# Attention and expert layer on one core: queries of head 0 issued ahead of two adjacency loads, and the shift rows and sums of unit 1 ahead of key copies

## The chip, the cores and the metric

The kernel runs on one core of a Trainium2 chip. The metric is the device time of one execution in microseconds (us). Five queues of instructions run side by side: TensorE (PE), VectorE (DVE), ScalarE (ACT), GpSimd (POOL) and SyncE (SP). They meet at semaphores only. SP does nothing here but wait for semaphores and issue DMAs, one after the other.

## The reference

The first half of the reference is a graph attention over 2048 nodes with 8 heads of 32 dimensions, masked by a 2048 x 2048 adjacency matrix:

```python
hs = layer_norm(h_source, ln1_scale, ln1_bias)
ht = layer_norm(h_target, ln1_scale, ln1_bias)
q = (ht @ Wq + bq).reshape(T, H, HD) / jnp.sqrt(jnp.float32(HD))
k = (hs @ Wk + bk).reshape(S, H, HD)
v = (hs @ Wv + bv).reshape(S, H, HD)
logits = jnp.einsum('thd,shd->hts', q, k)
logits = jnp.where(edge_mask[None] != 0, logits, NEG)
probs = jax.nn.softmax(logits, axis=-1)
ctx = jnp.einsum('hts,shd->thd', probs, v).reshape(T, D)
```

An output projection, a layer norm and a feed-forward layer follow, then a second residual layer that sends each node to two of eight experts. The change touches none of these.

## The kernel before

**Stages.** A front stage (0 to about 104 us) loads and normalises the inputs, turns them, and projects keys, queries and values in groups of 512 columns. Then 32 attention units run, one for a block of 512 target rows and a head: `n = 8 * b + h`. After them come projection, feed-forward and the experts.

**What a unit needs.** Queries and keys are kept as a high and a low part, stacked as three bands of 32 partitions, so that one matmul of 96 rows gives a score of nearly full precision: `ks` holds the keys of all heads, `qs` the queries of four units (a ring of 4). `piece` (L1575) computes scores target by source, from which DVE takes the row maxima (L973, with the mask `maskA`) and ACT the row sums (L1398). Maxima and sums of a unit are turned by TensorE (`turn_negmax`, L1584), split by DVE (`turned_shift`, L942 to L947), and stored by SP as two more rows of `qs`: `store_shift` (L433). Then `key_scores` (L1598, L1600) computes scores source by target with these rows as a bias and with the mask `maskB` added by a matmul with an identity, ACT takes the exponential (L1484), and `add_context` (L1612) multiplies by the values. The pieces of unit n+2 run between the key scores of unit n, and the key scores of a unit wait for its shift rows: `shift_rows[h % 4]` (L1590).

**SP's order.** It is written out by hand in `sync`: what stands late in it waits for everything before it. The helpers named below are:

- `stack_keys(h, cols, which)`: copies of 32 partitions from `kq_hi`, `kq_lo` into `ks` (L401).
- `stack_query(h)`: three copies of the queries of block 0 into `qs` (L407). The first for head 0 waits for `kq_split`, the ninth split by DVE (L920).
- `next_adjB(h)` and `load_adjB(b, h)`: 512 KB of the transposed adjacency into one of two buffers (L426). For h of 2 and more it waits until POOL has read the buffer: `maskB_next`.
- `store_queries`, `load_q`: queries of later blocks to DRAM and back (L414, L419).
- `store_shift`, `store_sums`, `load_inv`: the shift rows, the inverse sums to DRAM, and these back to 64 partitions (L433, L446, L454). `load_inv(n)` waits for `context_scaled >= n + 1`, POOL's multiplication for unit n-1.

In unit n the loop loads the queries of unit n+3, the adjacency of unit n+9 (after `maskB_next >= n + 8`), stores the context of unit n-2, and then does the three of unit n+1.

**POOL's order.** In unit n it makes the mask of block b+1 (`mask_b`, L725), scales the context of unit n-1 (L731), and prepares a chunk of the experts' weights (L700 to L712). `mask_b(1, 0)` waits for all key copies (`k_out`), because block 1's masks lie where the keys were made, and for its adjacency load.

Of the kernel before, what the change touches and what calls it, by code (L numbers as in the profile page):

```python
# [31 lines left out]
def graph_attention_and_experts(nc, x, adj, adjT, nodemask, h_target, ln1_scale, ln1_bias, Wq, bq, Wk, bk, Wv, bv,  # L32
                                Wo, bo, ln2_scale, ln2_bias, W1, W2, gate_wT, w1T, b1, w2T, b2, out):
    T, D = x.shape
    NT = T // P
    DC = D // P
    H = 8
# [5 lines left out]
    NG = NT // GT  # L43
    QSCALE = float(HD) ** -0.5
    KR = 3 * HD
    F = W1.shape[1]
    FC = F // P
    E, _, HE = w1T.shape
    HC = HE // P

    ctx = ExitStack()
    with ctx:
        def sem(name):
            return ctx.enter_context(nc.semaphore(name))
# [92 lines left out]
        kq_split = sem("kq_split")  # L147
# [51 lines left out]
        N = NB * H  # L199
# [28 lines left out]
        maskB_next = sem("maskB_next")  # L228
# [157 lines left out]
        with block:  # L386
            @block.sync
            def _(sp):
# [7 lines left out]
                def stack_keys(h, cols, which=(0, 1, 2)):  # L396
                    c, at_ = h // HPC, h % HPC * HD
                    for r in which:
                        part_ = (kq_hi, kq_lo, kq_hi)[r]
                        done = k_out[min(h, 2) if h < 4 or r == 1 else 3]  # L400
                        sp.dma_start(ks[r * HD:(r + 1) * HD, h, cols].bitcast(F32),  # L401
                                     part_[at_:at_ + HD, c, cols].bitcast(F32)).then_inc(done, 16)

                def stack_query(h):
                    at_ = h * HD
                    for r in range(3):
                        sp.dma_start(qs[r * HD:(r + 1) * HD, h, :].bitcast(F32),  # L407
                                     qq[at_:at_ + HD, 0, r // 2, 0, :].bitcast(F32)).then_inc(q_in[h], 16)

                def store_queries(g):  # L410
                    for c in range(DC):
                        sp.wait_ge(kq_split, DC * (NG + g) + c + 1)
                        for r, rows_ in enumerate((qh_rows, ql_rows)):
                            sp.dma_start(rows_[c * P:(c + 1) * P, g * GP:(g + 1) * GP],  # L414
                                         qq[:, g % 2, r, c, :].bitcast(F32)).then_inc(q_out[g % 2], 16)

                def load_q(n, b, h):
                    for r, rows in enumerate((q_high, q_high, q_low)):
                        sp.dma_start(qs[r * HD:(r + 1) * HD, h % 4, :].bitcast(F32),  # L419
                                     rows[h, :, bass.ds(b * TB, TB)]).then_inc(q_in[h % 4], 16)  # L420

                def load_adjA(tile, a):
                    sp.dma_start(adjA[:, a % 2, :], adj_t[tile, :, :]).then_inc(adjA_in[a % 2], 16)

                def load_adjB(b, h):
                    sp.dma_start(adjB[:, h % 2, :, :], adjT_t[:, 2 * h:2 * h + 2, bass.ds(b * TB, TB)])\  # L426
                        .then_inc(adjB_in[h % 2], 16)

                def store_shift(n, h):

                    sp.wait_ge(shift_split, n + 1)
                    for r, rows in enumerate((shift_hi, shift_lo)):
                        sp.dma_start(qs[KR + r:KR + r + 1, h % 4, :].bitcast(F32), rows[:, h % 2, :].bitcast(F32))\  # L433
                            .then_inc(shift_rows[h % 4], 16)

                def store_context(n, b, h):

                    wait_apart(sp, context_scaled, n + 2)
                    for half in range(2):
                        sp.dma_start(ctx_out[h, :, bass.ds(b * TB + half * (TB // 2), TB // 2)],  # L440
                                     total[half * HD:(half + 1) * HD, h % 2, :])\
                            .then_inc(context_out[h % 2], 16)

                def store_sums(n, h):
                    wait_apart(sp, inv_turned, n + 1)
                    sp.dma_start(inv_rows[bass.ds(n, 1), :].rearrange("o (a p) -> (o a) p", p=P),  # L446
                                 inv_sb[:, h % 2, :]).then_inc(sums_out[h % 2], 16)

                def load_inv(n, b, h):

                    sp.wait_ge(sums_out[h % 2], 16 * (b * (H // 2) + h // 2 + 2))
                    sp.wait_ge(context_scaled, n + 1)
                    for half in range(2):
                        sp.dma_start(rT[half * HD:(half + 1) * HD, :],  # L454
                                     inv_rows[bass.ds(n, 1), half * (TB // 2):(half + 1) * (TB // 2)]
                                     .rearrange("o t -> (o t)").partition_broadcast(HD)).then_inc(inv_in, 16)
# [14 lines left out]
                def load_h(b):  # L471
                    sp.dma_start(hb[:, b, :, :], ht_rows[b * TB:(b + 1) * TB, :]
                                 .rearrange("(a p) d -> p a d", p=P)).then_inc(hb_in[b], 16)
# [28 lines left out]
                def store_h(g):  # L502

                    sp.wait_ge(ht_ready, GT * (g + 1))
                    sp.dma_start(ht_t[:, GT * g:GT * (g + 1), :], hh[:, GT * g:GT * (g + 1), :]).then_inc(h_in[g], 16)

                def next_adjB(h):
                    if h < 2:
                        sp.wait_ge(hn_ready, NT)
                    else:  # L510
                        sp.wait_ge(maskB_next, h - 1)
                    load_adjB(0, h)
# [16 lines left out]
                stack_keys(0, group_cols(3))  # L529
                store_h(0)  # L530
                store_h(1)
                for h in range(2):
                    next_adjB(h)
                sp.wait_ge(kq_split, DC * NG + 1)
                stack_query(0)
                stack_keys(1, back_cols)
                stack_query(1)
                store_h(2)
# [18 lines left out]
                for n in range(N):  # L557
                    b, h = divmod(n, H)

                    if n + 3 < N:  # L560
                        sp.wait_ge(scores_ready, n * 8 + 1)
                        nb = (n + 3) // H
                        if n == 0:
                            sp.wait_ge(kq_split, 2 * DC * NG)
                            sp.wait_ge(v_stored, 2 * NG)
                        if (n + 3) % H == 0:
                            sp.wait_ge(q_out[nb % 2], 64 * (nb // 2 + 1))
                        load_q(n + 3, nb, (n + 3) % H)
                    if n == 0:
                        for h_ in range(4, H):  # L570
                            stack_keys(h_, slice(0, T), (0, 2))
                        sp.wait_ge(maskB_next, H - 1)
                        load_adjB(1, 0)
                    elif n < 3:
                        store_queries(n + 1)

                    if n + 1 + H < N:
                        sp.wait_ge(maskB_next, n + H)
                        load_adjB(*divmod(n + 1 + H, H))
                    if n > 1:  # L580
                        store_context(n - 2, *divmod(n - 2, H))
                    if n == H - 4:
                        for i in range(2):
                            sp.wait_ge(q_out[i], 128)
                    if h in (H - 4, H - 3) and b + 1 < NB:
                        for a in range(2 * (h - H + 4), 2 * (h - H + 5)):
                            sp.wait_ge(maskA_ready, TPB * (b + 1) + a - 1)
                            load_adjA((b + 1) * TPB + a, a)
                    if n + 1 < N:
                        store_shift(n + 1, (n + 1) % H)  # L590
                        store_sums(n + 1, (n + 1) % H)
                    load_inv(n, b, h)
                    if n == N - H:
                        sp.wait_ge(scores_ready, 8 * n)
                        load_constants()
                        sp.wait_ge(maskA_ready, TPB * NB)
                        load_h(0)
                        load_h(1)
                    elif n == N - H + 1:
                        load_h(2)  # L600
                        load_h(3)
                        sp.wait_ge(maskB_next, N)
                        load_context(0)
                        load_context(1)
                    elif n == N - 2:
                        sp.wait_ge(maxima_read, UNITS * N)
                        sp.wait_ge(whl_out, 16 * 4)
                        load_set(sp, ffn_w, 0, ffn_in)
                        sp.wait_ge(attn_ready, 2)
                        load_context(2)  # L610
# [1445 lines left out]
```

## Time and profile before

| | us |
|---|---|
| runs: median (lowest to highest of 3) | 1071.52 (1066.3 to 1072.51) |
| the profiled execution's own time | 1073.44 |
| span of the profile, first to last instruction | 1071.7 |
| mean granted TensorE clock | 0.947 |
| first piece of unit 0 | 70.00 |
| key scores of unit 0, 1, 2, 3 begin | 104.39, 124.65, 144.03, 160.47 |

The profile is one execution. Times in a timeline are counted from the start of its span. A row of a timeline gives start, duration, engine, line, operation, tiles, shape and count; in brackets stand the idle time of the engine before it and what ended that. Rows of SP are issues: how long issuing took, not the transfer. The clock column of the windows is the granted share of TensorE's full clock, 1.00 for 2.4 GHz and 0.50 for 1.2 GHz.

### The profile page before, as it was taken

What the parts mean: (1) busy time and instruction counts of PE and PEld (TensorE: products, weight loads), DVE (VectorE), ACT (ScalarE), POOL (GpSimd) and SP (SyncE); (2) the same over time, 40 slices, a digit from 0 to 9 for tenths busy, and PEclk for the clock granted to TensorE, in tenths of its full rate; (3) what the DMA queues carried; (4) which work ended last, traced back from release to release, by engine and by line L of the source; (5) the groups of instructions that cost most, each with busy time, mean ns of one, the idle gap of its engine ahead of it and who ended that gap; (6) DMA issues with size and microseconds to landing.
All of it is one profiled execution on the core that took longest, in us unless ns stands there. A gap on an engine that the chain in (4) does not pass through costs nothing. (4 is left out here: it accounts for less than half of the span.)

```text
span 1071.7 us, 20795 instructions
## 1 busy us (share of the span) xinstructions
PE 948.8 (89%) x6750; PEld 574.4 (54%) x6750; DVE 671.1 (63%) x1979; ACT 729.5 (68%) x917; POOL 540.6 (50%) x480
## 2 busy tenths in 40 slices
PE   2788999999999999999999988898930999999993
PEld 1355444444444444444444444464820898989873
DVE  6668587887878878788787745644643343434421
ACT  3536799899998999989999945653310645455551
POOL 6647486767667676676657972000453123232321
PEclk9899899999999999999999999998955999999997
DMA  9596766645366453664575464910542123232323
GB/s 282 157 268 179 203 213 224 232 156 179 120 220 240 160 180 118 218 242 142 167 265 194 143 217 141 421 63 21 207 173 73 40 44 62 43 59 40 47 38 94
DMA packets 74298, 168.43 MB, mean 157 GB/s; under 512 B 13586, under 2 KB 42386, under 8 KB 68242
## 3 DMA queue, kind: packets, MB, share of 16 engines
q1 hardware_dynamic: 50354, 97.99, 28.1%
q0 software_dynamic: 19984, 67.93, 21.0%
q10 hardware_dynamic: 3856, 1.19, 0.5%
q8 instruction: 58, 0.95, 0.4%
q14 instruction: 46, 0.38, 0.1%
HBM read 120.84 MB, written 61.96 MB: 171 GB/s over the span
## 5 line engine op out<-in xcount | busy, mean ns | idle before, releaser
L973 DVE CUSTOM_DVE_ANT_0 masked<-ps,maskA 128x512 f32<-128x512 f32 x512 | 346.5, 688 | 106.7 <-PE ps L1575 104.4
L1398 ACT ACTIVATE masked<-masked,negmax 128x2048 f32<-128x2048 f32 x128 | 256.7, 2005 | 33.8 <-DVE negmax L979 31.0
L1484 ACT ACTIVATE weights<-ps 128x1024 f32<-128x1024 f32 x256 | 248.7, 1010 | 32.3 <-PE ps L1600 31.9
L1575 PE MATMUL ps<-ks,qs 96*128 96x512 f32 x512 | 257.7, 537 | 13.2 <-DVE piecemax L973 9.0
L1598 PE MATMUL ps<-qs,ks 98*128 98x512 f32 x512 | 228.1, 505 | 2.4 <-DMA qs<-shift_lo 2.3
L1600 PE MATMUL ps<-maskB,identb 128*128 128x512 bf16 x512 | 202.8, 396 | 0.0
L1575 PEld LDWEIGHTS ps<-ks,qs 96*128 96x128 f32 x512 | 99.5, 194 | 96.7 <-DVE piecemax L973 75.8
L1876 POOL DMA_INDIRECT sum_rows<-y,ids x39 | 60.3, 1547 | 174.7 <-DVE y L1914 163.8
L1612 PE MATMUL ps<-weights,v_all 128*32 128x256 f32 x2048 | 137.7, 386 | 0.9 <-ACT weights L1484 0.9
L725 POOL TENSOR_SCALAR maskB<-adjB 128x1024 bf16<-128x1024 int32 x32 | 116.6, 3642 | 36.3 <-DMA adjB<-in_adjT 33.0
L1896 DVE TENSOR_TENSOR gT<-ffn_w,gT 128x2048 f16<-128x2048 f32 (+1 forms) x23 | 45.2, 1967 | 129.3 <-ACT gT L1953 129.3
L1600 PEld LDWEIGHTS ps<-maskB,identb 128*128 128x128 bf16 x512 | 50.4, 98 | 129.8 <-issue 127.3
L1988 PE MATMUL ps<-xT,wall 128*128 128x256 f16 (+1 forms) x1104 | 116.6, 260 | 0.2
L1598 PEld LDWEIGHTS ps<-qs,ks 98*128 98x128 f32 x512 | 101.4, 198 | 11.8 <-issue 3.4
L2000 PE MATMUL ps<-wall,gT 128*128 x936 | 106.2, 273 | 1.4 <-DVE y L1914 1.4
L1988 PEld LDWEIGHTS ps<-xT,wall 128*128 x1104 | 98.7, 98 | 15.7 <-issue 1.8
L1950 ACT ACTIVATE ffn_w<-ps,b1s 128x256 f32<-128x256 f32 (+1 forms) x184 | 70.9, 439 | 48.2 <-PE ps L1988 45.1
L2000 PEld LDWEIGHTS ps<-wall,gT 128*128 128x128 f16 x936 | 90.8, 98 | 13.4 <-issue 1.7
L731 POOL TENSOR_TENSOR total<-total,rT 64x256 f32<-64x256 f32 x32 | 23.4, 732 | 139.0 <-DVE total L961 138.9
L1612 PEld LDWEIGHTS ps<-weights,v_all 128*32 128x32 f32 x2048 | 53.6, 109 | 65.0 <-issue 41.4
L706 POOL TENSOR_TENSOR whl<-wch,whl 128x1024 f16<-128x1024 f32 x32 | 68.6, 2142 | 2.7
L1939 ACT ACTIVATE xT<-ps 128x512 f16<-128x512 f32 (+1 forms) x23 | 12.2, 532 | 77.0 <-PE ps L1975 77.0
(209 smaller groups left out, 1152.9 us busy)
## 6 DMA issues: line engine op xcount, KB each, us to landing
expert_rows<-pad_rows POOLq DMA_DIRECT2D x73, 272.0 KB, 5.9
split_weights<-whl POOLq DMA_DIRECT2D x36, 512.0 KB, 3.4
adjA<-in_adj SPq DMA_DIRECT2D x16, 1024.0 KB, 7.3
adjB<-in_adjT SPq DMA_DIRECT2D x32, 512.0 KB, 5.8
wall<-split_weights SPq DMA_DIRECT2D x16, 1024.0 KB, 15.8
wch<-in_w1T POOLq DMA_DIRECT2D x14, 512.0 KB, 5.9
wch<-in_w2T POOLq DMA_DIRECT2D x14, 512.0 KB, 6.2
xr<-expert_rows SPq DMA_DIRECT2D x16, 272.0 KB, 2.8
```

The costliest lines, as they stand in the source:

```text
L706: pool.tensor_tensor(whl[:, 1, :], chunk[:, :], whl[:, 0, :], ALU.subtract).then_inc(wch_split, 1)
L725: pool.tensor_scalar(maskB[:, b % 2, 2 * h:2 * h + 2, :], adjB[:, h % 2, :, :], 0.0, NO_EDGE, ALU.is_equal, ALU.mult).then_inc(maskB_next, 1)
L973: dve.tensor_tensor_reduce(masked[:, a % 2, k * 512:(k + 1) * 512], ps[:, u % 2, :], maskA[:, a, k * 512:(k + 1) * 512], 1.0, NO_EDGE, ALU ...
L1398: act.activation(masked[:, a % 2, :], masked[:, a % 2, :], ACT.Exp, bias=negmax[:, h % 2, a:a + 1], accum_out=rowsum[:, h % 4, a:a + 1]).t ...
L1484: act.activation(weights[:, j % 4, :, :], ps[:, 2 + 2 * (j % 2):4 + 2 * (j % 2), :], ACT.Exp).then_inc(weights_ready, 1)
L1575: pe.matmul(ps[:, u % 2, :], qs[0:KR, h % 4, a * P:(a + 1) * P], ks[0:KR, h, k * 512:(k + 1) * 512], start=True, stop=True)\
L1598: pe.matmul(bank, ks[:, h, (2 * j + i) * P:(2 * j + i + 1) * P], qs[:, h % 4, :], start=True, stop=False)
L1600: mm = pe.matmul(bank, identb[:, :], maskB[:, b % 2, 2 * j + i, :], start=False, stop=True)
L1612: mm = pe.matmul(ps[at:at + HD, 6 + h % 2, 0:TB // 2], v_all[:, 2 * j + i, h * HD:(h + 1) * HD], weights[:, j % 4, i, t * (TB // 2):(t + 1 ...
L1950: act.activation(g4[:, m, 0:w], ps[:, m // 2, m % 2 * PR:m % 2 * PR + w], ACT.Gelu, bias=b1s[:, e, m:m + 1], scale=1.0 / WSCALE).then_inc( ...
L1988: mm = pe.matmul(ps[:, m // 2, m % 2 * PR:m % 2 * PR + w], wall[:, e, 0, p, c * HE + m * P:c * HE + (m + 1) * P], xT[:, j % 2, x_, c, 0:w] ...
L2000: mm = pe.matmul(ps[:, 4 + a, 0:D], gT4[:, g, j % 2, m, a * P:(a + 1) * P], wall[:, e, 1, p, m * D:(m + 1) * D], start=(m == 0 and n == 0) ...
```

## The change

Two pieces of SP's written order move. The wait for the ninth split and the three query copies of head 0 go ahead of the first two adjacency loads. In the pass of the loop for unit 0, the eight full-width key copies of heads 4 to 7 and the two adjacency loads of block 1 go behind the shift rows, sums and inverse sums. Nothing is added or removed, and no other engine's order changes.

```diff
                 store_h(0)
                 store_h(1)
+                sp.wait_ge(kq_split, DC * NG + 1)
+                stack_query(0)
                 for h in range(2):
                     next_adjB(h)
-                sp.wait_ge(kq_split, DC * NG + 1)
-                stack_query(0)
                 stack_keys(1, back_cols)
...
-                    if n == 0:
-                        for h_ in range(4, H):
-                            stack_keys(h_, slice(0, T), (0, 2))
-                        sp.wait_ge(maskB_next, H - 1)
-                        load_adjB(1, 0)
-                    elif n < 3:
+                    if 0 < n < 3:
                         store_queries(n + 1)
 
-                    if n + 1 + H < N:
+                    if n and n + 1 + H < N:
                         sp.wait_ge(maskB_next, n + H)
                         load_adjB(*divmod(n + 1 + H, H))
...
                     load_inv(n, b, h)
+                    if n == 0:
+                        for h_ in range(4, H):
+                            stack_keys(h_, slice(0, T), (0, 2))
+                        for h_ in range(2):
+                            sp.wait_ge(maskB_next, H - 1 + h_)
+                            load_adjB(1, h_)
```

On SP, in the front stage, `ht_rows` is the store of the normalised targets, `adjB` the adjacency buffer and `qs<-qq` the query copies of head 0:

```order
 L401 DMA ks<-kq_hi 32x512
 L505 DMA ht_rows<-hh 128x4x256 x2
+L407 DMA qs<-qq 32x512 x3
 L426 DMA adjB<-in_adjT 128x2x512 x2
-L407 DMA qs<-qq 32x512 x3
 L401 DMA ks<-kq_hi 32x1024
 L401 DMA ks<-kq_lo 32x1024
```

The three query copies have changed places with the two adjacency loads.

On SP, in the loop's pass for unit 0, `turned_rows` and `shift_lo` are the shift rows of unit 1, `inv_rows` and `rT` its sums and those of unit 0 read back:

```order
 L419 DMA qs<-q_high 32x512 x2
 L419 DMA qs<-q_low 32x512
+L433 DMA qs<-turned_rows 1x4x128
+L433 DMA qs<-shift_lo 1x4x128
+L446 DMA inv_rows<-turned_rows 4x128
+L454 DMA rT<-inv_rows 32x256 x2
 L401 DMA ks<-kq_hi 32x2048 x8
 L426 DMA adjB<-in_adjT 128x2x512 x2
-L433 DMA qs<-turned_rows 1x4x128
-L433 DMA qs<-shift_lo 1x4x128
-L446 DMA inv_rows<-turned_rows 4x128
-L454 DMA rT<-inv_rows 32x256 x2
```

Five small transfers now stand ahead of eight copies of 256 KB and two loads of 512 KB; the load of the queries of unit 4 and the rest of the pass for unit 1 follow after both.

## Rows read from the trace of the kernel before

**Rows 1.** The page: busy time by engine, and the group of key-score matmuls.

```profile
PE 948.8 (89%) x6750; PEld 574.4 (54%) x6750; DVE 671.1 (63%) x1979; ACT 729.5 (68%) x917; POOL 540.6 (50%) x480
...
L1598 PE MATMUL ps<-qs,ks 98*128 98x512 f32 x512 | 228.1, 505 | 2.4 <-DMA qs<-shift_lo 2.3
```

**Rows 2.** Timeline of PE, last values of the front stage and first piece.

```profile
62.52 3.62 PE L1561 MATMUL ps<-w_v,sTx 128*128 128x256 f32 x16
70.00 0.76 PE L1575 MATMUL ps<-ks,qs 96*128 96x512 f32 x1 [3.87 <-DMA qs<-qq]
```

**Rows 3.** Windows: stretch, busy by engine (PE, PEld, DVE, ACT, POOL), clock, DMA share, GB/s.

```profile
70.00:74.00 4.00, 4.00 (x8) 2.07 (x9) 1.30 (x3) 0.30 (x1) 3.60 (x1) 0.62 1.06 388
124.65:131.00 6.35, 6.35 (x23) 3.00 (x27) 2.25 (x7) 3.74 (x4) 6.12 (x4) 0.50 0.43 143
```

**Rows 4.** Timeline of SP, the issues around the first query copies.

```profile
57.41 1.16 SPq L505 DMA_DIRECT2D ht_rows<-hh  x2
58.61 2.37 SPq L426 DMA_DIRECT2D adjB<-in_adjT  x2
61.02 1.84 SPq L407 DMA_DIRECT2D qs<-qq  x3
```

**Rows 5.** Timeline of DVE: the splits of the first queries, and unit 1's shift rows.

```profile
60.07 1.40 DVE L920 SCALAR_TENSOR_TENSOR qq<-ps,bkq,qq 128x512 fp32r<-128x512 f32 x2
...
117.85 0.28 DVE L944 TENSOR_TENSOR shift_lo<-ps,turned_rows 4x128 fp32r<-4x128 f32 x1
```

**Rows 6.** Line L401, 55.5 to 57.4 us: three key copies of 32x512.

```profile
DMA to landing us min/median/max: 1.9/2.1/2.1
```

**Rows 7.** Line L505, 57.4 to 58.6 us: the two stores just ahead.

```profile
DMA to landing us min/median/max: 3.2/3.9/4.6
```

**Rows 8.** Timeline of POOL: masks of block 0 and 1, scaling of unit 0.

```profile
90.07 3.63 POOL L725 TENSOR_SCALAR maskB<-adjB 128x1024 bf16<-128x1024 int32 x1 [3.35 <-DMA adjB<-in_adjT]
...
104.93 3.63 POOL L725 TENSOR_SCALAR maskB<-adjB 128x1024 bf16<-128x1024 int32 x1 [2.47 <-DMA adjB<-in_adjT]
...
123.31 3.63 POOL L725 TENSOR_SCALAR maskB<-adjB 128x1024 bf16<-128x1024 int32 x1 [14.08 <-DMA adjB<-in_adjT]
...
137.80 0.73 POOL L731 TENSOR_TENSOR total<-total,rT 64x256 f32<-64x256 f32 x1
```

**Rows 9.** Timeline of PE: key scores, last of unit 0, first of units 0 to 3.

```profile
104.39 0.63 PE L1598 MATMUL ps<-qs,ks 98*128 98x512 f32 x1
...
119.56 0.39 PE L1598 MATMUL ps<-qs,ks 98*128 98x512 f32 x1
...
124.65 0.80 PE L1598 MATMUL ps<-qs,ks 98*128 98x512 f32 x1 [2.34 <-DMA qs<-shift_lo]
...
144.03 0.39 PE L1598 MATMUL ps<-qs,ks 98*128 98x512 f32 x1
...
160.47 0.40 PE L1598 MATMUL ps<-qs,ks 98*128 98x512 f32 x1
```

**Rows 10.** Timeline of SP, units 0 to 2.

```profile
107.65 8.26 SPq L401 DMA_DIRECT2D ks<-kq_hi  x8
115.96 2.51 SPq L426 DMA_DIRECT2D adjB<-in_adjT  x2
118.51 0.64 SPq L433 DMA_DIRECT2D qs<-turned_rows  x1
...
120.41 0.79 SPq L454 DMA_DIRECT2D rT<-inv_rows  x2
...
129.99 0.66 SPq L426 DMA_DIRECT2D adjB<-in_adjT  x1
140.01 0.59 SPq L433 DMA_DIRECT2D qs<-turned_rows  x1
...
145.16 0.77 SPq L419 DMA_DIRECT2D qs<-q_high  x2
...
156.44 0.59 SPq L433 DMA_DIRECT2D qs<-turned_rows  x1
```

## Prediction

> **What bounds the kernel now.** I read the page first, for the engine that is busy nearly always: TensorE, 89% of the span, so time is lost or won where it stands still. The same rows say that all 512 key-score matmuls together waited 2.3 us for shift rows [rows 1]. That is one wait in one place, not a tax on every unit. Then I went along TensorE's timeline for gaps ended by a DMA. There are two at the places of the change. The values of the front stage end at 62.52 + 3.62 = 66.14 us and the first piece starts at 70.00, after 3.87 us of idling for the query copies [rows 2]. The first key scores of unit 1 start at 124.65 after 2.34 us for the shift rows [rows 9]. After each gap the engine ran at the low level: the granted clock is 0.62 on average from 70 to 74 us, and 0.50 (1.2 GHz) from 124.65 to 131 us [rows 3]. Third, I read SP's timeline beside those of DVE and POOL, since the change moves SP's issues alone, and asked of every moved issue what it waits for and who waits behind it.
>
> **Part 1: the query copies.** Before, SP issues two stores, two adjacency loads and then the copies, at 61.02 [rows 4]. What the change takes away is not issue time. The copies wait for the first of two splits that DVE starts at 60.07 and ends together at 61.47 [rows 5], so for about 60.8. SP, free at 58.6, waits until then and issues the copies from 60.8 to 62.6, 0.2 us earlier than before. What they are spared is the 1 MB of adjacency ahead of them in the queue. Copies of the same shape with little ahead landed in 2.1 us [rows 6]: 62.0 + 2.1 = 64.1. The two stores ahead landed at most 4.6 us after issue, by about 62.7 [rows 7]. Both are before 66.14, so the wait of 3.87 us should go whole. The slow clock behind it should go too: 4.0 us at 0.62 lose 1.5 us. Together 5.4 us.
>
> What is late next? The two adjacency loads now start at 62.7 instead of 58.6, and all else on SP shifts with them. Masks of block 0 are made from these loads. The last one was done at 104.93 + 3.63 = 108.6, and the last key scores of unit 0 that read it ran at 119.56 [rows 8, 9], so 11 us cover 5.4 + 4.1. The tighter cover is the shift rows of unit 0: SP issues them behind an adjacency load that waits for the fifth mask, done at 90.07 + 3.63 = 93.7 [rows 8]. From the issue of shift rows to the first key scores the later units take 4.0 us (140.01 to 144.03, 156.44 to 160.47) [rows 9, 10]. Key scores that begin 5.4 us earlier than 104.39, at 99.0, want that issue at 95.0. With 0.4 us for the load, the fifth mask may be 0.9 us later than now. If it were the full 4.1 us late, only 2.2 us would be left (5.4 - 4.1 + 0.9); if not late, 5.4. The DMA engines are full around 70 to 74 us (share 1.06) [rows 3], so landings there go by bytes queued ahead, which are the same for the later loads, and not by issue. I therefore take a gain of 5.0 us, between 2.2 and 5.4.
>
> **Part 2: the shift rows of unit 1.** Before, DVE ends them at 118.13 [rows 5] and SP issues them at 118.51, hardly late. They suffer from the queue: 3 MB issued from 107.65 on [rows 10]. Unit 1's key scores start 6.1 us after the issue instead of 4.0. What this costs now: 2.34 us of waiting, and a slow unit behind it. From unit 1 to unit 2 it is 19.38 us, from unit 2 to unit 3 16.44 [rows 9], so 2.94 us. Sum 5.3 us, which the change removes in unit 1.
>
> But it also moves ten transfers past these rows, and all that SP issues next stands behind them. I follow it on the times of before, with part 1's shift left out since it moves both sides alike. SP issues the shift rows at 118.2 and, after the 2.7 us that this block takes (118.51 to 120.41 + 0.79), the key copies from 120.9. Before, POOL's first mask of block 1 started 15.7 us after the first copy (107.65 to 123.31, after 14.08 us of waiting for its load) [rows 8, 10]. So now it starts at 136.6 and ends at 140.2. SP meanwhile loads and stores queries and comes to the next adjacency load, which needs the buffer that this mask reads. Before it was issued at 129.99 with the mask long done; now SP stands there until 140.2. Behind it in SP's order stand the shift rows of unit 2, which are ready a unit's 16.44 us after those of unit 1, at 134.6. They go out after the load's issue of 0.66 us, at 140.9, and key scores can begin 4.0 us later, at 144.9. TensorE, no longer stopped in unit 1, would be there at 122.31 + 16.44 = 138.75. A new wait of 6.2 us takes the place of the old 2.34, one unit later, and I expect the same slow clock behind it, 2.94 us. New cost 9.1, old cost 5.3: part 2 loses 3.8 us.
>
> Its bounds: if the rows have to wait behind a full queue as unit 1's did, 6.1 us instead of 4.0, the wait is 8.3 us and the loss 6.0. If copies and first load, 2.6 MB, moved at 388 GB/s, the rate of 70 to 74 us [rows 3], plus 2.1 us for landing, the mask would start 8.9 us after the first copy, at 129.8. SP would reach the shift rows at 134.1, before they are ready, and the gain would be 5.3. The rate is known for just these copies, though, by 15.7 us; I stay with it.
>
> The Trainium skill, "DMA: Bandwidth & Descriptors", section "Queues, rings and completion order", says that each DMA engine takes descriptors in the order of its queue's ring, though transfers need not complete in order of issue. The trace agrees on the first half, by the 6.1 us in unit 1 against 4.0 later. By that rule unit 2's rows also stand behind the stored queries and the load just issued: 8.3 us of wait and a time 2.1 us above mine. Rows that slip past the queue give mine.
>
> Two things I cost at nothing. The copies must have landed before the pieces of unit 4, which run beside unit 2; TensorE reaches these right after the key scores that wait anyway. The sums and their reading back move earlier and nobody waited for them.
>
> **Sum.** 5.0 - 3.8 = 1.2 us less than the profiled execution's 1073.44, so 1072.2. That execution is 1.9 us above the median of the runs, 1071.52; against the median it is 1070.3. A measurement of this kernel can tell about 1% (10.7 us) from no change, and this is far inside.
>
> **The rivals.**
>
> *A: both waits go.* SP gets past the masks in time, as in the lower bound above. For it speaks the rate of 388 GB/s that the queue did reach [rows 3], against it the 15.7 us of the same transfers [rows 8, 10]. Gain 5.0 + 5.3 = 10.3: 1061.2.
>
> *B: the delay goes on into unit 3, and the kernel is slower.* POOL scales unit 0's context 14.5 us after the start of that mask (123.31 to 137.80), ending at 138.5 [rows 8]. With the mask at 136.6 it ends at 151.8, and SP's reading back of unit 1's sums waits for that. SP then loads the queries of unit 5 at 152.6 instead of 145.16. From there to the key scores of unit 3 it was 15.3 us [rows 9, 10], which would be 167.9, while TensorE wants them at 144.9 + 2.94 + 16.44 = 164.3. At most 3.6 us of wait and again 2.94 of slow clock, 6.5 in all: 1.2 - 6.5 = -5.3, 1076.8. It decides if more than 11.7 of the 15.3 us are needed. Against it: no wait stood in unit 3, so some of the 15.3 is slack, and POOL's own transfers come later than these.
>
> *C: part 1 gives little.* The fifth mask comes the full 4.1 us late, and unit 0 waits for its shift rows. For it: 4.1 us are how far the loads really move, and every mask hangs on the one two before. Against it: the full queue. Gain 2.2, loss 3.8: 1073.1.
>
> **How the numbers follow.** The forecast has 0.56: a net between +3.7 (a gain of 5.4, a wait of 4.0) and -2.0 (a gain of 4.0, a wait of 8.3), 1067.8 to 1073.5. A has 0.16, B 0.16, C 0.12. The range of 8 in 10 reaches down towards A and up into B: 1062.5 to 1076.5. Faster by over 1% needs 1060.8 or less, which is A with a little more: 0.06. Slower by over 1% needs 1082.2, beyond B: 0.02. Within 1%: 0.92.
>
> **What would show it.** Step by step in the profile after: the first piece right behind the values, with no gap ended by `qs<-qq` and a clock of 1.00 after it; the first key scores of unit 1 without a gap; POOL idle for over 20 us before block 1's first mask; SP's second load of block 1 in the loop held by POOL; and a gap of about 6 us ended by `shift_lo` before the key scores of unit 2, with the clock at 0.50 behind it. It is wrong if that gap is missing or under 3 us, if unit 0 waits for its shift rows, or if units 3 and 4 show gaps of their own.

## The result, and the profile after

The changed kernel takes 1076.12 us (median of 15 runs) and the kernel before 1067.71 us (15 runs beside it). The ratio is 1.0073, with a 95% interval of 1.0057 to 1.0089: slower by 0.73%, or 7.8 us. (The medians lie 8.4 us apart; the ratio leaves out one far longer run of each kernel, 3541 us before and 1371 us after.) The forecast was 1.2 us faster: the time lies 0.4 us inside the stated range of 1062.5 to 1076.5, but the kernel went the other way. A difference of 0.73% was clear of the noise, where the prediction took 1% for the least that can be told.

The two profiled executions do not show 7.8 us: their spans are 1071.7 us before and 1072.5 us after. The one before took 1073.44 us, 5.7 more than its median, the one after 1074.22, 1.9 less than its own. Part of this is where they begin to count. The values of the front stage, which the change does not touch, start at 58.19 us in the one and at 55.98 in the other, and over all the profiles of this study anywhere from 55.5 to 58.5. I therefore count from the first value matmul. In TensorE's timeline of the kernel before these rows were not shown yet:

```profile
58.19 3.62 PE L1561 MATMUL ps<-w_v,sTx 128*128 128x256 f32 x16
...
176.89 0.40 PE L1598 MATMUL ps<-qs,ks 98*128 98x512 f32 x1
```

The first is the start of the values, the second that of the key scores of unit 4: 118.70 us. The same timeline of the changed kernel, with what answers to [rows 2] and [rows 9]:

```profile
55.98 3.62 PE L1562 MATMUL ps<-w_v,sTx 128*128 128x256 f32 x16
60.31 3.62 PE L1562 MATMUL ps<-w_v,sTx 128*128 128x256 f32 x16
63.58 0.58 PE L1576 MATMUL ps<-ks,qs 96*128 96x512 f32 x1
...
85.56 1.47 PE L1576 MATMUL ps<-ks,qs 96*128 96x512 f32 x2 [4.86 <-DVE piecemax L974]
...
102.90 0.86 PE L1599 MATMUL ps<-qs,ks 98*128 98x512 f32 x2
...
119.49 0.40 PE L1599 MATMUL ps<-qs,ks 98*128 98x512 f32 x1
...
142.29 0.80 PE L1599 MATMUL ps<-qs,ks 98*128 98x512 f32 x1 [6.22 <-DMA qs<-shift_lo]
...
163.79 0.51 PE L1599 MATMUL ps<-qs,ks 98*128 98x512 f32 x1 [2.07 <-DMA qs<-shift_lo]
...
181.81 0.40 PE L1599 MATMUL ps<-qs,ks 98*128 98x512 f32 x1
```

From 55.98 to 181.81 it is 125.83 us, 7.1 more than before. That agrees with the 7.8 us of the ratio, so the loss lies in this stretch. (Behind unit 4 the profiled execution after ran 4.1 us shorter than the one before, 890.7 against 894.8 us to the end of the span; with the early start of 2.2 us this is why the spans look alike. No line that the change moves runs there, and over the twelve profiles of this study this rest takes 889.7 to 896.1 us without following the edits: 890.7 also with part 1 alone.)

Both gaps of [rows 2] and [rows 9] that the change was aimed at are gone: the first piece stands right behind the values, and unit 1 starts without a bracket, that is without a wait. Three others have come: 4.86 us in unit 0 itself, 6.22 before unit 2 and 2.07 before unit 3. The page has the last two in one group, where before stood 2.3 us [rows 1]:

```profile
L1599 PE MATMUL ps<-qs,ks 98*128 98x512 f32 x512 | 227.6, 504 | 8.3 <-DMA qs<-shift_lo 8.3
```

The windows of the changed kernel show the clock behind these four places (columns as in [rows 3]):

```profile
63.60:80.00 16.40, 15.41 (x48) 7.83 (x46) 12.78 (x34) 7.62 (x9) 9.33 (x3) 1.00 1.05 308
85.60:92.00 6.40, 6.40 (x18) 4.81 (x19) 4.36 (x13) 3.17 (x5) 3.63 (x1) 0.63 0.89 184
142.30:148.50 6.20, 6.20 (x23) 2.98 (x27) 2.25 (x7) 3.61 (x4) 5.83 (x6) 0.51 0.66 209
163.80:168.00 4.20, 4.20 (x19) 1.98 (x23) 1.85 (x6) 2.72 (x2) 3.75 (x4) 0.70 0.29 61
```

Behind the gap that went the clock is 1.00 where it was 0.62. Behind each of the three new ones it is below full: 0.63, 0.51, 0.70.

**Where the front's gain went.** Part 1 did what the prediction says, and the time came back 20 us later. This is ScalarE in the changed kernel, at the line that puts the high part of a query group into `qq`:

```profile
74.64 0.69 ACT L1392 ACTIVATE qq<-ps,bkq 128x512 fp32r<-128x512 f32 x1 [2.27 <-issue]
77.21 0.67 ACT L1392 ACTIVATE qq<-ps,bkq 128x512 fp32r<-128x512 f32 x1
83.43 0.69 ACT L1392 ACTIVATE qq<-ps,bkq 128x512 fp32r<-128x512 f32 x1 [5.55 <-DMA q_low<-qq]
```

`qq` has two buffers. Groups 2 and 3 overwrite those of groups 0 and 1, and `high_part` waits until the stores of these (L414 before, `store_queries(0)` and `store_queries(1)`) have landed. DVE stops behind ScalarE, and TensorE behind DVE, the 4.86 us above:

```profile
84.15 0.75 DVE L921 SCALAR_TENSOR_TENSOR qq<-ps,bkq,qq 128x512 fp32r<-128x512 f32 x1 [4.00 <-ACT qq L1392]
```

In the kernel before, the same instruction of group 3:

```profile
85.05 0.69 ACT L1391 ACTIVATE qq<-ps,bkq 128x512 fp32r<-128x512 f32 x1 [0.43 <-PE ps L1549]
```

It waited for TensorE alone, but only just. SP issued these stores at 77.80 to 80.04, and by the view of line 414 of the kernel before, 77.7 to 80.5 us, they landed so:

```profile
DMA to landing us min/median/max: 3.4/4.0/4.3
```

The last was down by 80.04 + 4.3 = 84.3 at the latest, some 0.7 us before it was needed. In the changed kernel the same view, 73.5 to 76.2 us, reads:

```profile
  ACT qq L1392: 5.5, 1
...
DMA to landing us min/median/max: 7.3/7.5/7.7
```

The stores are issued 3.8 to 4.8 us earlier (73.51 to 75.64) and take 3.5 us longer. What stands ahead of them in the queue, adjacency, keys and queries, is the same number of bytes as before. Counted from the first value they land 27.4 us after it (83.4), before 26.1 (84.3). ScalarE, on the other hand, was ready for the buffer at 83.43 - 5.55 = 77.88, which is 21.9 us after the first value instead of 26.9: a pull forward of 5 us ran into a margin of 0.7.

**What happened in the loop.** Here is SP in the changed kernel (before: [rows 10]):

```profile
115.49 0.59 SPq L433 DMA_DIRECT2D qs<-turned_rows  x1
...
118.13 8.28 SPq L401 DMA_DIRECT2D ks<-kq_hi  x8
126.45 2.48 SPq L426 DMA_DIRECT2D adjB<-in_adjT  x2
...
138.46 0.38 SPq L426 DMA_DIRECT2D adjB<-in_adjT  x1
138.89 0.64 SPq L433 DMA_DIRECT2D qs<-turned_rows  x1
...
157.54 0.59 SPq L433 DMA_DIRECT2D qs<-turned_rows  x1
```

and POOL (before: [rows 8]):

```profile
134.80 3.63 POOL L726 TENSOR_SCALAR maskB<-adjB 128x1024 bf16<-128x1024 int32 x1 [26.61 <-DMA adjB<-in_adjT]
...
154.67 0.77 POOL L709 DMA_DIRECT2D split_weights<-whl  x1 [0.30 <-POOL whl L707]
155.37 0.87 POOL L697 DMA_DIRECT2D wch<-in_L_gnn_W  x1
156.15 1.13 POOL L713 DMA_DIRECT2D expert_rows<-pad_rows  x2
```

The chain of part 2 is there link by link. The load for POOL's first mask of block 1 comes late; POOL idles 26.61 us and ends that mask at 138.43; SP stands until then before its next adjacency load (5.4 us, by its waits), out at 138.46; unit 2's rows follow at 138.89 and TensorE waits 6.22 us for them. Unit 3 is another case. Its rows went out at 157.54 with SP waiting for DVE, not DVE for SP:

```profile
SPq L433 <- DVE shift_lo L945: 1.5, 1, 1.5
```

(SP's waits, 151 to 160 us.) But the key scores came 6.25 us later instead of about 4. Two things stand closer ahead of these rows than before. POOL, late by its mask, had just issued its own 1.57 MB from 154.67: a store and a load of 512 KB and two fills of 272 KB. Before, the transfers of that round went out at 144.53, 12 us ahead of those rows. And SP, which had stood 9.3 us for POOL's scaled context (until 150.09), issued its own load of 512 KB at 154.22, 3.3 us ahead of the rows; before it was 149.01 and 156.44, 7.4 us. No run separates the two for unit 3; e8 below shows that POOL's transfers can do it, for unit 2 of another kernel.

### The profile page after: what moved, and what is told of

It reads as the page before. It is cut to its first block and busy times, and to the rows that moved or that the text cites. A ratio compares the mean times of both kernels' runs of the same rounds, so it can differ in the third digit from the quotient of the medians.

```text
span 1072.5 us, 20731 instructions
## 1 busy us (share of the span) xinstructions
PE 944.7 (88%) x6686; PEld 573.2 (53%) x6750; DVE 672.0 (63%) x1979; ACT 729.8 (68%) x917; POOL 541.5 (50%) x480
## 5 line engine op out<-in xcount | busy, mean ns | idle before, releaser
L1601 PE MATMUL ps<-maskB,identb 128*128 128x512 bf16 x448 | 177.5, 396 | 0.0
```

The costliest lines, as they stand in the source:

```text
L1601: mm = pe.matmul(bank, identb[:, :], maskB[:, b % 2, 2 * j + i, :], start=False, stop=True)
```

## The experiments

All runs compute everything; only SP's order, and in one case a wait of POOL, differ. Two measures are given for each: the ratio of times to the kernel before, with its 95% interval, and from the profile the stretches by which theories can be told apart. A unit without a gap takes 16.43 us. The stretches come from one profiled execution of each kernel.

| kernel | ratio (95%) | values to key scores of unit 0 | units 0, 1, 2, 3 | values to unit 4 |
|---|---|---|---|---|
| before | 1 | 46.20 | 20.26, 19.38, 16.44, 16.42 | 118.70 |
| changed | 1.0073 (1.0057 to 1.0089) | 46.92 | 16.59, 22.80, 21.50, 18.02 | 125.83 |
| e1 part 1 alone | 1.0013 (0.9995 to 1.0032) | 48.96 | 20.14, 16.50, 16.41, 16.42 | 118.43 |
| e2 part 2 alone | 1.0104 (1.0084 to 1.0124) | 47.68 | 17.11, 22.33, 20.70, 18.00 | 125.82 |
| e3 e1 + stores ahead | 0.9963 (0.9950 to 0.9977) | 41.94 | 21.20, 19.22, 16.45, 16.43 | 115.24 |
| e4 only loads behind | 0.9999 (0.9980 to 1.0018) | 47.50 | 16.59, 18.33, 19.59, 16.43 | 118.44 |
| e5 e3 + e4 | 0.9936 (0.9912 to 0.9960) | 41.44 | 17.28, 16.46, 17.67, 16.50 | 109.36 |
| e7 changed, unit 2's rows ahead | 1.0084 (1.0059 to 1.0108) | 47.07 | 16.59, 19.40, 24.14, 18.96 | 126.16 |
| e8 e4, POOL's transfers held | 1.0060 (1.0033 to 1.0086) | 47.42 | 16.60, 16.43, 25.00, 18.56 | 124.02 |
| e9 e3, unit 0's rows ahead | 0.9961 (0.9943 to 0.9979) | 40.36 | 22.45, 19.22, 16.43, 16.42 | 114.87 |
| e10 e5, unit 0's rows ahead | 0.9927 (0.9899 to 0.9954) | 40.35 | 17.98, 19.45, 16.50, 16.43 | 110.70 |
| e11 changed + stores ahead | 1.0037 (1.0022 to 1.0052) | 41.92 | 17.95, 22.63, 21.53, 16.50 | 120.52 |

With the front as it was (before, e2, e4, e8) the first column varies from 46.20 to 47.68, so a difference of 1.5 us there says nothing.

**e1 and e2: one part each.**

```diff
 e1 = before, and
+                sp.wait_ge(kq_split, DC * NG + 1)
+                stack_query(0)
                 for h in range(2):
                     next_adjB(h)
-                sp.wait_ge(kq_split, DC * NG + 1)
-                stack_query(0)
 e2 = before, and the rest of the change (the loop)
```

> The first half of the change alone: head 0's query copies ahead of the two adjacency loads, unit 0 of the loop as before. Theory: the gap of 3.87 us before the first piece goes, but ScalarE then waits longer for the second pair of query stores (q_low, 5.5 us in the changed kernel), because the bytes queued ahead of these stores are the same. Key scores of unit 0 begin 38 to 39.5 us after the first piece (34.4 before), and the time is within 2 us of before. Rival (the half keeps its 5 us and the whole loss is the other half's): 5 us faster than before, key scores of unit 0 begin 33 us after the first piece.

> The second half alone: shift rows and sums of unit 1 ahead of key copies and block 1's first loads, the front stage as before. Theory: no wait before unit 1, 6 us before unit 2, about 2 us before unit 3, and the low clock behind them; 6 to 7 us slower than before. Rival (the wait in unit 3 came from the first half's shift of SP's work, so this half costs only the 3.8 us that were forecast): 3 to 4.5 us slower, no wait before unit 3.

e1 takes as long as before, 1068.30 against 1067.33 us, as expected. Its ScalarE shows where the 5 us went, without any help of part 2:

```profile
83.91 0.69 ACT L1391 ACTIVATE qq<-ps,bkq 128x512 fp32r<-128x512 f32 x1 [5.40 <-DMA q_low<-qq]
```

It is the same wait for the store of group 1. One expectation was missed: unit 0 begins 41.36 us after the first piece, not 38 to 39.5. By the table the front even lost 2.8 us in this profile, and unit 1, whose wait was followed by a full clock this time (last section), gave 2.9 back. e2 has the changed kernel's 125.8 us with the front as before, and the same two new gaps on TensorE:

```profile
144.30 0.80 PE L1599 MATMUL ps<-qs,ks 98*128 98x512 f32 x1 [5.75 <-DMA qs<-shift_lo]
...
165.00 0.51 PE L1599 MATMUL ps<-qs,ks 98*128 98x512 f32 x1 [1.84 <-DMA qs<-shift_lo]
```

So part 1 alone neither gains nor loses, and part 2 alone loses as much as the whole or more: 1.0104 is 11 us, where 6 to 7 were expected. The halves add to 1.0117 and the whole is 1.0073. In the stretch up to unit 4 e2 loses the 7.1 us of the whole and no more; where its other 4 us lie was left open. The waits before units 2 and 3 do not need part 1, so the rival of e2, which put unit 3 down to the front, is out.

**e3 and e11: is it the stores?** If the wait for `qq` took part 1's gain, stores that go ahead of the bulk must give it back.

```diff
                 stack_query(1)
-                store_h(2)
                 store_queries(0)
-                store_h(3)
+                store_queries(1)
+                store_h(2)
                 next_adjB(2)
                 stack_keys(2, back_cols)
+                store_h(3)
                 next_adjB(3)
-                store_queries(1)
                 stack_keys(3, back_cols)
```

e3 is e1 with this, e11 the changed kernel with it.

> The first half of the change, and the stores of query group 1 moved up directly behind those of group 0, ahead of two stores of normalised targets, two adjacency loads and the key copies of head 2. Theory (bytes queued ahead of the query stores hold ScalarE): ScalarE's wait for q_low falls from 5.5 us to under 1, key scores of unit 0 begin 33 to 35 us after the first piece, and the kernel is 4 to 5 us faster than before. Rival (the masks, whose loads come later still, or the DMA engines' total bytes bound the stretch): the wait turns up at the shift rows of unit 0 or at the masks, at most 1 us faster than before.

> The changed kernel with the stores of query group 1 moved up as in the kernel with the stores ahead; the loop as changed. Theory (front stage and loop are separate losses: the front's 5 us come back, the loop's waits before units 2 and 3 stay): 1 to 4 us slower than before, ScalarE's wait for q_low under 1 us, waits of 5 us or more before unit 2. Rival (the loop's waits come from the front's lateness): as fast as before or faster, no wait over 3 us before unit 2.

ScalarE in e3 at the two places:

```profile
75.01 0.69 ACT L1391 ACTIVATE qq<-ps,bkq 128x512 fp32r<-128x512 f32 x1 [0.54 <-PE ps L1549]
...
79.37 0.69 ACT L1391 ACTIVATE qq<-ps,bkq 128x512 fp32r<-128x512 f32 x1 [0.42 <-PE ps L1549]
```

No wait for a store is left, unit 0 begins 41.94 us after the values instead of 46.20, and the kernel is faster than before, 0.9963, interval below 1. On top of the changed kernel the same edit takes 1.0073 down to 1.0037, and the waits before units 2 and 3 stay, 6.05 and 1.80 us: front and loop are separate losses. This shows the cause in part 1. With the stores out of the way the next wait shows, 1.43 us for unit 0's shift rows in e3 and 1.41 in e11:

```profile
100.03 0.76 PE L1598 MATMUL ps<-qs,ks 98*128 98x512 f32 x1 [1.43 <-DMA qs<-shift_lo]
```

In e3 the fifth mask ended at 95.99 (before: 93.70), the adjacency load that waits for it went out at 96.02, and the rows behind it at 96.45. That is the place that rival C named.

**e4 and e5: part 2 without its chain.** Only the two loads go behind the rows; the key copies stay ahead, so the first mask of block 1 starts at 123.25, as before (123.31), and not at 134.80.

```diff
                     if n == 0:
                         for h_ in range(4, H):
                             stack_keys(h_, slice(0, T), (0, 2))
-                        sp.wait_ge(maskB_next, H - 1)
-                        load_adjB(1, 0)
...
-                    if n + 1 + H < N:
+                    if n and n + 1 + H < N:
...
                     load_inv(n, b, h)
+                    if n == 0:
+                        for h_ in range(2):
+                            sp.wait_ge(maskB_next, H - 1 + h_)
+                            load_adjB(1, h_)
```

e5 is e3 with this loop.

> The loop as before, but only block 1's first two adjacency loads go behind the shift rows; the eight key copies stay ahead of them. Theory (the 1 MB of adjacency is what held unit 1's shift rows, and the mask is early enough when the key copies are issued early): no wait before unit 1 and none before unit 2, block 1's first mask starts about 126 us, SP is not held at the next load; 4 to 5.5 us faster than before. Rival (the key copies hold the shift rows): a wait of 1.5 us or more before unit 1 stays, at most 2 us faster.

> Both of the last two edits together: head 0's queries and the stores of query group 1 ahead in the front stage, block 1's first two loads behind unit 1's shift rows, the key copies ahead of them. Theory (each edit acts in its own place, and in the loop a wait of about 1.8 us moves from unit 1 to unit 2): 3 to 5 us faster than before. Rival (with SP's order free of late waits both gains add): 8 us faster or more.

I missed on e4, which was to be 4 to 5.5 us faster and takes the time of before. The gap before unit 1 is gone and SP is not held by the mask (unit 2's rows go out at 132.81), but a wait before unit 2 stands there all the same:

```profile
120.38 0.40 PE L1600 MATMUL ps<-qs,ks 98*128 98x512 f32 x1
...
138.71 0.80 PE L1600 MATMUL ps<-qs,ks 98*128 98x512 f32 x1 [1.75 <-DMA qs<-shift_lo]
```

5.9 us from issue to key scores, not 4.0. POOL's timeline in e4 has something that stands beside the issue:

```profile
131.65 0.75 POOL L710 DMA_DIRECT2D split_weights<-whl  x1 [0.30 <-POOL whl L708]
132.35 0.59 POOL L698 DMA_DIRECT2D wch<-in_L_gnn_W  x1
132.91 1.04 POOL L714 DMA_DIRECT2D expert_rows<-pad_rows  x2
```

The rows of 2 KB were issued at 132.81, in the middle of POOL's 1.57 MB. In e5, where both edits together shift the phases, the rows of unit 2 go out ahead of POOL's transfers and only small waits are left:

```profile
99.93 1.15 PE L1600 MATMUL ps<-qs,ks 98*128 98x512 f32 x2 [0.93 <-DMA qs<-shift_lo]
...
117.22 0.50 PE L1600 MATMUL ps<-qs,ks 98*128 98x512 f32 x1 [0.31 <-DMA qs<-shift_lo]
...
151.35 0.50 PE L1600 MATMUL ps<-qs,ks 98*128 98x512 f32 x1 [1.06 <-DMA qs<-shift_lo]
```

e5 takes 1061.13 us against 1068.42: 7 us faster than before, and faster than the changed kernel. That is more than the 3 to 5 us expected and less than the 8 of the rival. Its interval overlaps that of e3; what the loads add to e3 shows in the stretch, 109.36 us against 115.24, in one profile of each.

**e8: is it POOL's transfers?** e4, with POOL held before that round's transfers until unit 2's rows have landed.

```diff
                     pool.wait_ge(wch_in, 16 * (n + 1))
+                    if n == 0:
+                        pool.wait_ge(shift_rows[2], 32)
                     split(i, wch)
```

> The kernel of the loads behind the shift rows, and GpSimd's work on the first weight chunk (whose store, next load and two fills of padding rows, 1.6 MB, were issued within 2.3 us just before unit 2's shift rows) is held until these rows have landed. Theory (GpSimd's burst is what delayed the rows): no wait before unit 2, 0.3 us at most; GpSimd's lag then shows at the sums of unit 1 and can give a wait before unit 3; 0 to 4 us faster than before. Rival (SP's own stores of queries hold the rows): the wait of 1.75 us before unit 2 stays.

Unit 1 now takes an undisturbed 16.43 us, with no wait before unit 2, where e4 had 1.75: for e4's unit 2 the cause is shown. But POOL stood 7.99 us for it and its later transfers came at 151.31, just ahead of unit 3's rows at 152.65:

```profile
161.78 0.79 PE L1602 MATMUL ps<-qs,ks 98*128 98x512 f32 x1 [8.41 <-DMA qs<-shift_lo]
```

The same collision, one unit later and dearer; here SP's own queries, stores and a load of 512 KB, issued from 147.59 on after a wait for POOL, stand just ahead of the rows too. The kernel is slower, 1.0060, where 0 to 4 us faster was expected.

**e7: is unit 2's wait SP standing before the gated load?** The changed kernel, with unit 2's rows and sums ahead of the adjacency load that waits for the mask.

```diff
+                    if n == 1:
+                        store_shift(2, 2)
+                        store_sums(2, 2)
                     if n and n + 1 + H < N:
                         sp.wait_ge(maskB_next, n + H)
                         load_adjB(*divmod(n + 1 + H, H))
...
-                    if n + 1 < N:
+                    if n != 1 and n + 1 < N:
                         store_shift(n + 1, (n + 1) % H)
```

> The changed kernel, with the shift rows and sums of unit 2 also put ahead of the adjacency load that waits for block 1's first mask; nothing else moved. Theory (SP stands at that load while the rows are ready, and GpSimd's lag holds the reading back of the sums after it): the wait before unit 2 falls from 6.2 us to 3.5 or less, a wait of 1 to 3 us before unit 3 stays, 3 to 6 us slower than before. Rival (the rows wait in the DMA queue behind key copies, query loads and stores, whatever SP does): the wait before unit 2 stays at 5 us or more, 7 us slower or more.

The rows leave at 133.09, 4.7 us ahead of the load, and TensorE shows:

```profile
138.94 0.79 PE L1602 MATMUL ps<-qs,ks 98*128 98x512 f32 x1 [2.84 <-DMA qs<-shift_lo]
...
163.09 0.79 PE L1602 MATMUL ps<-qs,ks 98*128 98x512 f32 x1 [4.89 <-DMA qs<-shift_lo]
```

Over half of the 6.22 us goes, so standing behind the gated load was a cause. The 2.84 us left I put down to the queue, without a run that shows it: the rows took 5.85 us from issue to use, and the bulk ahead of them was still landing, as POOL's wait for its load shows.

```profile
134.16 3.63 POOL L729 TENSOR_SCALAR maskB<-adjB 128x1024 bf16<-128x1024 int32 x1 [25.89 <-DMA adjB<-in_adjT]
```

Yet unit 3's wait grows from 2.07 to 4.89 and the sum stays, 1.0084 against 1.0073 with overlapping intervals, where 3 to 6 us slower and 1 to 3 us before unit 3 were expected. Unit 3's rows now leave at 155.42, 1.4 us after the start of POOL's issues at 154.03, where the changed kernel had 2.9 us between them.

**e9 and e10: unit 0's rows ahead of an adjacency load, for the 1.43 us that e3 left.**

```diff
-                next_adjB(6)
                 store_shift(0, 0)
                 store_sums(0, 0)
+                next_adjB(6)
```

e9 is e3 with this, e10 is e5 with it.

> The kernel with the query stores ahead, and the shift rows and sums of unit 0 ahead of the seventh adjacency load of block 0. Theory (512 KB just ahead of these rows cause the 1.4 us of wait before unit 0): that wait goes, 5 to 8 us faster than before. Rival (the rows wait for the fifth mask's loads or the stretch is bound elsewhere): the wait stays at 1 us or more and the time is that of the kernel with the query stores ahead, 4 us faster.

> The fastest kernel so far (query stores ahead, loads behind unit 1's rows), and the shift rows and sums of unit 0 ahead of the seventh adjacency load. Theory (a wait that is removed without taking bytes out of the queue comes back at the next rows): unit 0 starts 1 us sooner after the first piece, a wait of 1 to 3 us turns up before unit 1 or 2, and the time is that of the kernel without this edit, 6 to 8 us faster than before. Rival (each wait is its own): 9 us faster or more.

Unit 0's wait is gone in both, so standing behind that load, which waits for the fifth mask, was its cause; and neither gains anything measurable over e3 (0.9961 against 0.9963) or e5 (0.9927 against 0.9936). In e9 the 2.96 us before unit 1 has become:

```profile
118.67 0.80 PE L1598 MATMUL ps<-qs,ks 98*128 98x512 f32 x1 [5.71 <-DMA qs<-shift_lo]
```

Unit 1's rows still stand behind the same 3 MB. Arriving earlier only makes the wait longer. In e10 new waits of 1.58 and 1.26 us stand before units 1 and 2, as expected; in e9 the 5 to 8 us expected did not come.

## Why the prediction was wrong

By its own steps, in the order of its parts:

1. **"The wait of 3.87 us should go whole", and the slow clock with it: right.** SP was free at 57.35, waited for the split as reckoned, and issued the copies at 58.64; the first piece follows the values with a clock of 1.00. From the start of the values to the first piece it is 7.60 us instead of 11.81, 4.2 less.

2. **"What is late next?": the step that failed.** It tested two covers, the masks of block 0 and the shift rows of unit 0, and in the changed kernel both held: no wait stands before unit 0. (The second held only because the stores stopped the stage first; with these ahead it is short by 1.43 us, in e3.) It did not ask which instruction waits for the completion of a store that SP issues later in the same queue. The guard of `qq` is in `high_part`, and its row in the trace before says that ScalarE idled 0.43 us for TensorE and none for the store, which looks like ease and was 0.7 us from a wait. The "gain of 5.0 us, between 2.2 and 5.4" was measured as none, since 4.86 us of waiting with a clock of 0.63 behind it took back what the 3.87 us had given: 46.92 against 46.20 us to unit 0, and e1's time within 0.32% of before. e3 and e11 show the cause. The argument that landings "go by bytes queued ahead" was even in the text, for the loads; it was not carried on to the stores, to which it applied just so. Of the miss this is the larger part: 5.0 + 0.7 = 5.7 us in the stretch to unit 0.

3. **Rival C was nearer in size but had another place.** It left part 1 a gain of 2.2 us and wanted unit 0 to wait for its shift rows after a late fifth mask. No such wait came in the changed kernel. It came in e3 and e11, 1.4 us, once the stores no longer stopped the stage first.

4. **Part 2, unit 1: right, and a little too small.** The rows went out early and the gap is gone. The gain was put at 2.34 + 2.94 us. Unit 0's own length also fell, from 20.26 to 16.59, 3.67 us where the gap explains 2.34, so 1.3 us more were won than counted. They are the clock: in the first 6.1 us of unit 0 it was 0.50 before (104.40 to 110.50) and 0.72 after (102.90 to 109.00), and 6.1 * 0.22 = 1.3. The prediction did not count this, and no run shows what caused it.

5. **Part 2, unit 2: right, link by link.** POOL idle over 20 us: 26.61. SP held at the next load, 5.4 us, until the mask was done. A wait of 6.2 us: 6.22. Slow clock behind it, 2.94: unit 2 is 21.50 - 16.43 - 2.07 = 3.00 us too long at a clock of 0.51. The rows took 142.29 - 138.89 = 3.40 us from issue to use, below the 4.0 taken, though the load went out just before them. On the other side they were issued 2.8 us after TensorE was ready (136.07 to 138.89), where the forecast had 2.15; that the wait fits to 0.1 us is two errors of 0.6 that cancel. By the ring rule of the Trainium skill, "DMA: Bandwidth & Descriptors", section "Queues, rings and completion order", the prediction had a wait of 8.3 us as another way; it did not come: these rows, behind one load of 512 KB, showed no delay.

6. **Unit 3: the forecast left it out.** By the prediction's own signs a gap there made it wrong. Rival B had the place, and a price of at most 3.6 us of wait and 2.94 of slow clock; measured were 2.07 and, by unit 3's length of 18.02, 1.6. Its mechanism is half of what the rows show. B made SP late by its wait for POOL's context, and SP did stand 9.3 us there, which put its own load 3.3 us ahead of the rows instead of 7.4. But at 157.54 SP was waiting for DVE: the rows were issued in time, and what came late was their landing, with POOL's transfers beside them too. e8 shows for e4's unit 2, where SP's last load was 5.9 us ahead of the rows (126.91 to 132.81), that a wait came or went with POOL's transfers; for unit 3 the shares are open. Against B the prediction said "POOL's own transfers come later than these". They come with POOL, and the moved mask made POOL late by 11.5 us (123.31 to 134.80), which put the round that used to start at 144.53 to 154.67. The Trainium skill says of this, in the same page under "Issuing engines are not separate DMA queues", that transfers started by different engines run on the same DMA engines and interleave. The 5.9 us in e4, where the rows stand in SP's queue and the bulk in POOL's, agree. B's time, 1076.8, came near the measured 1076.12 by luck: it holds part 1's gain of 5.0 us, which did not come, and a price of unit 3 that was too high.

**Rival A** (both waits go) fell with point 5: POOL's first mask came 16.7 us after the first key copy (118.13 to 134.80), near the 15.7 taken and far from the 8.9 that A needed.

**The sum.** The four units from key scores of unit 0 to those of unit 4 grew from 72.50 to 78.91 us, 6.4 instead of the 3.8 of part 2: 3.7 more in unit 3, 1.3 less by point 4, and 0.2 of small differences. With 0.7 in the front this makes the 7.1 us. Part 2's bound was a loss of 6.0, part 1's did not allow zero.

**The distance to unit 3** is worth a look across the runs. Take the time from POOL's first issue of a round to the shift rows behind it, and TensorE's wait for them: 2.9 us and 2.07 (changed, unit 3), 1.4 and 4.89 (e7, unit 3), 1.3 and 8.41 (e8, unit 3), 1.2 and 1.75 (e4, unit 2), 4.2 and 1.06 (e5, unit 3). Rows that go out before the round (e5, unit 2) or 8 us after it (before, [rows 9, 10]: 140.01, no wait) do not wait. The size is not a function of the distance alone, since SP's own bytes differ; which part each has was not separated.

## What to carry to other kernels

When a transfer is pulled forward, look for what waits for the completion of later stores in the same queue (the guards of buffers about to be overwritten), and work out the margin in the trace before as landing against use, since a row without a wait may be half a microsecond from one. Here a small transfer was not helped by going ahead of bulk that feeds another engine: that engine's lag moved its own transfers and SP's, and the wait appeared again at the next small transfer (e7, e8). Even without that lag the next rows met the same bulk (e9). What paid here: part 1 with the stores that free a buffer ahead of the bulk (e3, 0.9963), and with it only the two loads behind the rows (e5, 0.9936).

## What was not expected of the hardware

A gap of the same length did not always cost the clock. In e1 TensorE waits before unit 1 a little longer than before [rows 9], 2.58 us against 2.34:

```profile
124.61 0.49 PE L1598 MATMUL ps<-qs,ks 98*128 98x512 f32 x1 [2.58 <-DMA qs<-shift_lo]
...
141.11 0.40 PE L1598 MATMUL ps<-qs,ks 98*128 98x512 f32 x1
```

Before, the clock behind it was 0.50 [rows 3] and the unit took 19.38 us. In e1 the window reads 1.00, and the unit 16.50:

```profile
124.60:131.00 6.40, 6.39 (x38) 3.22 (x39) 3.62 (x12) 4.92 (x5) 6.17 (x4) 1.00 0.46 154
```

A second pair shows the same. e4 waits 1.75 us before unit 2 and then takes 19.59 us for it; e11 waits 1.80 before unit 3 and takes 16.50. These are the windows behind the two waits, e4 first:

```profile
138.70:145.00 6.30, 6.29 (x23) 3.00 (x27) 2.25 (x7) 3.68 (x4) 5.85 (x6) 0.50 0.41 144
159.85:166.10 6.25, 6.25 (x36) 3.19 (x37) 3.51 (x11) 4.78 (x5) 5.79 (x7) 1.00 0.48 140
```

So "the same slow clock behind it, 2.94 us" was one of at least two outcomes of such a gap. The gap of 6.22 us met the dear one, which the one row of the trace before could not tell. What decides was not tried. The other surprise is the scatter of the front stage: the values of an unchanged front begin up to 3 us apart between executions, 0.3% of the span, so a difference of this size between two profiles has to be read stage by stage.
